# Two rows sent to all partitions through scratch memory instead of through diagonals and products with ones, in a decoder layer of 16 sequences

## The reference

```python
x = layernorm(x + linear_attention(x))                 # 16 heads of 32, elu+1, causal cumulative sums
x = layernorm(x + channel_attention(q=x, k=ctx, v=ctx))
x = layernorm(x + expert_ffn(x))                       # one of 8 experts for each sequence, 512 -> 2048 -> 512
# channel_attention, 4 heads of 128 channels, for (global, local):
scores = einsum('bhdn,bhen->bhde', (q*wq + bq) heads, (k*wk + bk) heads) * 512**-0.5
attn = softmax(scores)                                 # 128 x 128 per head
out += einsum('bhde,bhen->bhdn', attn, (v*wv + bv) heads)
result = 2 * out * wp + bp
```

## Time and profile before

| | |
|---|---|
| median of 3 runs | 2603.87 us (2602.91 to 2604.93) |
| profiled execution | 2608.33 us |
| its span | 2606.6 us |
| TensorE busy | 2471.1 us, 95% |
| VectorE busy | 1751.3 us, 67% |
| ScalarE busy | 1172.8 us, 45% |
| GpSimd busy | 532.9 us, 20% |
| mean granted TensorE clock | 0.979 |

### The profile page before, as it was taken

One profiled execution on the slowest core, in us unless ns is written; L12 is line 12 of the kernel. 1 busy time (PEld: TensorE's weight loads), 2 busy tenths in 40 slices (PEclk: granted clock), 3 DMA queues, 4 the chain that ended last, 5 costly groups with the idle time before them and its releaser, 6 DMA issues.

```text
span 2606.6 us, 33240 instructions
## 1 busy us (share of the span) xinstructions
PE 2471.1 (95%) x11584; PEld 1988.0 (76%) x11584; DVE 1751.3 (67%) x2721; ACT 1172.8 (45%) x1920; POOL 532.9 (20%) x452
## 2 busy tenths in 40 slices
PE   6866899999999999999999999999999999999998
PEld 5654678878787787878878787887878778777876
DVE  6667576677767667676767768667776766765443
ACT  4323444534444453554544454354444445354443
POOL 3132212122122212211221122212212221222110
PEclk9977999999999999999999999999999999999999
DMA  7323343433434344343433434343343434222331
GB/s 270 121 97 110 125 143 112 136 134 118 155 103 169 102 137 150 103 150 116 154 117 125 143 124 154 113 143 125 114 157 111 157 109 147 94 89 82 109 109 65
DMA packets 83400, 331.85 MB, mean 127 GB/s; under 512 B 11810, under 2 KB 11810, under 8 KB 72738
## 3 DMA queue, kind: packets, MB, share of 16 engines
q1 hardware_dynamic: 83234, 329.72, 36.6%
HBM read 306.61 MB, written 23.07 MB: 126 GB/s over the span
## 4 chain that ended last, share of the span: by engine, by line
PE 85%; DVE 9%; issue 3%; ACT 2%; DMA 1%; POOL 0%; SPq 0%; ACTq 0%; DVEq 0%; POOLq 0%
PE m L870 27%; PE h_ps L870 25%; PE acc L1047 24%; DVE junk_v L724 2%; PE m L1005 2%; PE m L946 2%; DVE a_v L728 2%; PE m L1021 1%; PE m L918 1%; PE m L953 1%; DVE h_lo L770 1%; PE m L994 1%; ACT rden_all L508 1%; DVE rden L609 1%; DVE we_lo L762 0%
## 5 line engine op out<-in xcount | busy, mean ns | idle before, releaser
L870 PE MATMUL m<-xT_hi,wq 128*128 128x512 f32 x1536 | 522.3, 404 | 25.0 <-DVE wq L552 10.7
L426 ACT ACTIVATE we_hi<-raw 128x1024 fp32r<-128x1024 f32 x256 | 271.1, 1059 | 517.8 <-PE acc L1047 512.7
L762 DVE TENSOR_TENSOR we_lo<-raw,we_hi 128x1024 fp32r<-128x1024 f32 x256 | 368.7, 1440 | 187.1 <-ACT we_hi L426 187.1
L1047 PE MATMUL acc<-we_hi,h_hi 128*128 128x512 f32 x1024 | 425.7, 416 | 0.4
L870 PE MATMUL h_ps<-x2T_hi,we_hi 128*128 128x512 f32 x1024 | 409.0, 399 | 5.9 <-DVE x2T_lo L756 5.9
L870 PE MATMUL h_ps<-x2T_lo,we_hi 128*128 128x512 f32 x1024 | 405.0, 395 | 0.0
L870 PE MATMUL h_ps<-x2T_hi,we_lo 128*128 128x512 f32 x1024 | 404.9, 395 | 0.0
L1047 PE MATMUL acc<-we_hi,h_lo 128*128 128x512 f32 x1024 | 404.7, 395 | 0.0
L1047 PE MATMUL acc<-we_lo,h_hi 128*128 128x512 f32 x1024 | 404.3, 395 | 0.0
L436 ACT ACTIVATE hid<-h_ps,b 128x512 f32<-128x512 f32 x256 | 175.6, 686 | 475.6 <-PE h_ps L870 475.6
L870 PEld LDWEIGHTS m<-xT_hi,wq 128*128 128x128 f32 x1536 | 294.6, 192 | 98.9 <-issue 27.4
(11 more groups left out here) (126 smaller groups left out, 3486.1 us busy)
## 6 DMA issues: line engine op xcount, KB each, us to landing
raw<-in_w SPq DMA_DIRECT2D x256, 512.0 KB, 3.8
wq<-wq_scratch SPq DMA_DIRECT2D x180, 512.0 KB, 3.3
xT_raw<-in_xT SPq DMA_DIRECT2D x16, 1024.0 KB, 5.8
x<-in_x_tok SPq DMA_DIRECT2D x16, 1024.0 KB, 5.5
ctx_tok<-in_ctx_tok SPq DMA_DIRECT2D x16, 1024.0 KB, 4.8
ctx_T<-in_ctxT SPq DMA_DIRECT2D x16, 1024.0 KB, 4.9
out_dram<-x SPq DMA_DIRECT2D x16, 1024.0 KB, 4.8
wq_scratch<-wq SPq DMA_DIRECT2D x12, 512.0 KB, 4.5
```

Of the source, the lines that this page charges most:

```text
L426: act.activation(we_hi[:, g % NW, :], raw[:, g % NR, :], ACT.Copy).then_inc(whi_done, 1)
L762: dve.tensor_tensor(we_lo[:, g % NW, :], raw[:, g % NR, :], we_hi[:, g % NW, :].bitcast(F32), ALU.subtract).then_inc(wlo_done, 1)
L870: last = pe.matmul(out, lhsT, rhs, start=(n == 0), stop=(n == 3 * len(pairs) - 1))
L1047: last = pe.matmul(acc[t][:, :], hx[:, f % 2, ts], wx[:, g % NW, C:], start=(f == 0 and n == 0), stop=(f == FC - 1 and n == 2))
```

## The change

The two rows take another way. `c_col` and `k_all2` are each stored by SP, element by element, as a row of 512 in DRAM scratch, and read back with one broadcast DMA to all 128 partitions, into `c_sb` and `const_b`. The diagonals on GpSimd, the two products with ones on TensorE and ScalarE's two copies out of PSUM go. ScalarE's four sums move from h = 4 to h = 1. SP gets a store at h = 2 and a read at h = 4 for the sums, a store at h = 18 and a read at h = 20 for the constants. The waits follow.

```diff
--- before.py
+++ after.py
@@ -53,6 +53,9 @@
+    c_dram = nc.dram_tensor("c_scratch", [1, XH * P], F32, kind="Internal").ap()
+    k_dram = nc.dram_tensor("k_scratch", [1, XH * P], F32, kind="Internal").ap()
     with ExitStack() as ctx:
@@ -95,7 +98,6 @@
         c_sb = sb("c_sb", [P, XH, P])
-        diag = sb("diag", [P, XH, P])
         s_x, s_q = sb("s_x", [P, XH]), sb("s_q", [P, 2, XH])
@@ -149,12 +151,12 @@
         x1_done, x2_done, norm_done = sem("x1_done"), sem("x2_done"), sem("norm_done")
-        g_mm, sx_mm, c_mm, cb_done = sem("g_mm"), sem("sx_mm"), sem("c_mm"), sem("cb_done")
-        csum_done, diag_done, sx_done, sq_done = sem("csum_done"), sem("diag_done"), sem("sx_done"), sem("sq_done")
+        g_mm, sx_mm, c_st, c_in = sem("g_mm"), sem("sx_mm"), sem("c_st"), sem("c_in")
+        csum_done, sx_done, sq_done = sem("csum_done"), sem("sx_done"), sem("sq_done")
         sc_done, max_done, nmax_done, exp_done = sem("sc_done"), sem("max_done"), sem("nmax_done"), sem("exp_done")
         rec_done, rec2_done, av_done = sem("rec_done"), sem("rec2_done"), sem("av_done")
-        asum_done, kall_done, kall2_done, diag2_done = (sem(n) for n in ("asum_done", "kall_done", "kall2_done", "diag2_done"))
-        aT_mm, kb_mm, aT_done, kb_done, x1c_done = (sem(n) for n in ("aT_mm", "kb_mm", "aT_done", "kb_done", "x1c_done"))
+        asum_done, kall_done, kall2_done = (sem(n) for n in ("asum_done", "kall_done", "kall2_done"))
+        aT_mm, k_st, aT_done, k_in, x1c_done = (sem(n) for n in ("aT_mm", "k_st", "aT_done", "k_in", "x1c_done"))
         out_mm, res2_done = sem("out_mm"), sem("res2_done")
@@ -217,6 +219,31 @@
                             load_job(a + 1, j + NQ - JOBS)
+                    if h == 2 and inside(c):
+                        sp.wait_ge(csum_done, XH * c + XH)
+                        if (due := upto(c - 1, 16, 16)) is not None:
+                            sp.wait_ge(c_in, due)
+                        sp.dma_start(c_dram[0].rearrange("(h p) -> p h", p=P), c_col[:, :], allow_slow_non_contiguous=True).then_inc(c_st, 16)
+                    if h == 4 and inside(c):
+                        sp.wait_ge(c_st, 16 * c + 16)
+                        if (due := upto(c - 1, 12, 4)) is not None:
+                            sp.wait_ge(sc_done, due)
+                        sp.dma_start(c_sb[:, :, :].rearrange("p h e -> p (h e)"), c_dram.broadcast_to([P, XH * P])).then_inc(c_in, 16)
+                    if h == 18 and inside(c):
+                        sp.wait_ge(kall2_done, c + 1)
+                        if (due := upto(c - 1, 16, 16)) is not None:
+                            sp.wait_ge(k_in, due)
+                        sp.dma_start(k_dram[0].rearrange("(h p) -> p h", p=P), k_all2[:, :], allow_slow_non_contiguous=True).then_inc(k_st, 16)
+                    if h == 20 and inside(c):
+                        sp.wait_ge(k_st, 16 * c + 16)
+                        sp.wait_ge(csum_done, XH * c + XH)
+                        if (due := upto(c - 1, TT, TT)) is not None:
+                            sp.wait_ge(x1c_done, due)
+                        sp.dma_start(const_b[:, :], k_dram.broadcast_to([P, C])).then_inc(k_in, 16)
                     if h == 11 and inside(z):
@@ -309,10 +336,6 @@
-            def diagonal(col, done):
-                pool.tensor_tensor(diag[:, :, :], ident[:, :].unsqueeze(1).broadcast_to([P, XH, P]),
-                                   col[:, :].unsqueeze(2).broadcast_to([P, XH, P]), ALU.mult).then_inc(done, 1)
             for i in range(NB + 4):
@@ -321,12 +344,6 @@
                                        b2[:, 0:1, :].broadcast_to([P, TT, C]), ALU.add).then_inc(b2_done, 1)
-                if inside(c):
-                    pool.wait_ge(csum_done, XH * c + XH)
-                    if (due := upto(c - 1, 1, 1)) is not None:
-                        pool.wait_ge(kb_mm, due)
-                    diagonal(c_col, diag_done)
                 if inside(e):
@@ -340,11 +357,7 @@
                 if inside(c):
-                    pool.wait_ge(kall2_done, c + 1)
-                    pool.wait_ge(c_mm, c + 1)
-                    diagonal(k_all2, diag2_done)
-                    pool.wait_ge(kb_done, c + 1)
+                    pool.wait_ge(k_in, 16 * c + 16)
@@ -444,6 +457,18 @@
                     split_x2(b, 3)
+                if h == 1 and inside(c):
+                    act.wait_ge(ctxT_in, 16 * c + 16)
+                    if (due := upto(c - 1, 16, 16)) is not None:
+                        act.wait_ge(c_st, due)
+                    if (due := upto(c - 1, TT, TT)) is not None:
+                        act.wait_ge(x1c_done, due)
+                    for hd in range(XH):
+                        if (due := upto(c, XH, hd)) is not None:
+                            act.wait_ge(csum_done, due)
+                        act.activation(const_b[:, :], ctx_T[:, hd, :], ACT.Copy,
+                                       accum_out=c_col[:, hd:hd + 1]).then_inc(csum_done, 1)
                 if i == 0 and h in JOB_AT:
@@ -454,24 +479,6 @@
                     normalise(1, e)
-                if h == 4 and inside(c):
-                    act.wait_ge(ctxT_in, 16 * c + 16)
-                    if (due := upto(c - 1, 1, 1)) is not None:
-                        act.wait_ge(diag_done, due)
-                    if (due := upto(c - 1, TT, TT)) is not None:
-                        act.wait_ge(x1c_done, due)
-                    for hd in range(XH):
-                        if (due := upto(c, XH, hd)) is not None:
-                            act.wait_ge(csum_done, due)
-                        act.activation(const_b[:, :], ctx_T[:, hd, :], ACT.Copy,
-                                       accum_out=c_col[:, hd:hd + 1]).then_inc(csum_done, 1)
-                if h == 5 and inside(c):
-                    act.wait_ge(c_mm, c + 1)
-                    if (due := upto(c - 1, 12, 4)) is not None:
-                        act.wait_ge(sc_done, due)
-                    act.activation(c_sb[:, :, :], by_head, ACT.Copy).then_inc(cb_done, 1)
                 if h == 7 and inside(c):
@@ -515,11 +522,6 @@
                     high_part(a, 1)
-                if h == 21 and inside(c):
-                    act.wait_ge(kb_mm, c + 1)
-                    act.wait_ge(csum_done, XH * c + XH)
-                    act.activation(const_b[:, :], M2[:, :], ACT.Copy).then_inc(kb_done, 1)
                 if h == 22 and inside(a):
@@ -674,7 +676,7 @@
             def scores_ctx(c):
-                dve.wait_ge(cb_done, c + 1)
+                dve.wait_ge(c_in, 16 * c + 16)
                 for v, bq in enumerate((BQG, BQL)):
@@ -732,8 +734,8 @@
                         dve.wait_ge(kall_done, c + 1)
-                        if (due := upto(c - 1, 1, 1)) is not None:
-                            dve.wait_ge(diag2_done, due)
+                        if (due := upto(c - 1, 16, 16)) is not None:
+                            dve.wait_ge(k_st, due)
                         dve.tensor_tensor(k_all2[:, :], k_all[:, :], cols[:, BP, :], ALU.add).then_inc(kall2_done, 1)
@@ -946,16 +948,10 @@
-            def ctx_sums(c):
-                pe.wait_ge(diag_done, c + 1)
-                pe.wait_ge(sc_done, 12 * c + 2)
-                pe.matmul(by_head, ones[:, :], diag[:, :, :], start=True, stop=True).then_inc(c_mm, 1)
             def x_sums(c):
-                pe.wait_ge(cb_done, c + 1)
+                pe.wait_ge(sc_done, 12 * c + 2)
                 for h in range(XH):
@@ -987,18 +983,10 @@
-            def constants(c):
-                pe.wait_ge(diag2_done, c + 1)
-                pe.wait_ge(aT_done, c + 1)
-                pe.matmul(by_head, ones[:, :], diag[:, :, :], start=True, stop=True).then_inc(kb_mm, 1)
             def attend(c, t):
                     pe.wait_ge(ctxT_in, 16 * c + 16)
-                    pe.wait_ge(kb_done, c + 1)
                 else:
@@ -1059,8 +1047,6 @@
                     gram(c)
-                if h == 5 and inside(c):
-                    ctx_sums(c)
                 if h == 7 and inside(c):
@@ -1078,8 +1064,6 @@
                     spread_reciprocal(a, 2 * (h - 20) + 1)
-                if h == 21 and inside(c):
-                    constants(c)
                 if 23 <= h <= 26 and inside(a):
```

## The result

The changed kernel takes 2627.19 us (median of 6 runs, 2624.24 to 2630.08) against 2604.4 us for the kernel before (6 runs, 2601.99 to 2610.7). The ratio is 1.0082, 95% interval [1.0068, 1.0096]: slower by 0.8%. The forecast was 2561, with a range of 2543 to 2583.

A forecast was written before the change was run, and what follows sets the result against it. TensorE was taken as the bound, busy 2471.1 of 2606.6 us and 85% of the chain. Products 24.8, edges 16.7 and projection wait 2 summed to 43.5, say 43 us gained: 2561 us, range 2543 to 2583.

The forecast's parts named there:

- the queue: DMA queue: two 256 KB reads and two 2 KB stores add 3% an iteration, no chain engine waiting there; cost nothing.
- the store's price: Store of 512 single elements: 5 us to landing, bounds 3.9 and 21.2; may take 12 us before anything is late.
- Rival 3: Late element store delays VectorE's residual 2 and TensorE; slower, 2678 us, deciding from about 15 us of store; chance 0.09.
- stays above 153.3: Sign in the profile after: a steady period above 153.3 us, not 152.5, means freed time is partly given back.
- rival 1: GpSimd's adds hit more VectorE low parts, TensorE waits at the projection; 20 us gained, 2584 us; chance 0.13.
- The rule of the Trainium skill: At the element stores: a strided last dimension becomes one descriptor per element, here 512, making the 21.2 us bound the one to watch.
- Products with ones: Two TensorE products removed from the steady iteration: 1.05 and 0.86 us, 24.8 us gained over 13 iterations.
- ScalarE's sums in half step 1: Four ScalarE sums, 3.0 us, moved from half step 4 into 4.30 us of idle time; cost nothing.
- The contention at the low parts: GpSimd's adds beside VectorE's low parts: the 1.53 us wait before the projection stays nearly; 0.2 us an iteration, 2 in all.
- rival 2: The constants' row comes early enough that GpSimd's adds no longer collide with VectorE; 67 us gained, 2537 us; chance 0.07.
- Edges: Iterations i = 1, 2 and 16: diagonal waits and products go; 16.7 us gained, ends 6.2 and 21.9.
- GpSimd loses two diagonals, off the chain: GpSimd: the two removed diagonals were taken as off the chain, with no gain put on them.

The follow-up runs named there:

- kernel 7: Changed kernel with both stores' 512 single elements written 64 bytes apart and the rows read from an input, not scratch; 2555.41 us.
- kernel 1: Changed kernel with both stores as 128 runs of 16 bytes instead of 512 single elements, rows permuted; 2555.98 us, ratio 0.9805 to the kernel before.
- kernel 3: Changed kernel with only the constants through scratch; the sums keep diagonal, product and copy, ScalarE's sums stay at half step 4; 2675.67 us.
- kernel 4: Changed kernel with both element stores issued by ScalarE on its own queue, the reads staying with SP; 2628.2 us, ratio 1.0089 to the kernel before.
- kernels 2 to 5: Changed kernel with only sums through scratch (2584.34 us), only constants (2675.67), stores on ScalarE's queue (2628.2), stores on GpSimd's queue (2619.4).
- kernel 6: Changed kernel, but TensorE transposes the columns to four rows, ScalarE copies them behind its query features, stores write four 512 B runs; 2603.78 us.

## Why the prediction was wrong

**The step that failed is the sentence on *the queue***: "in a stretch where no engine on the chain waits for a load: nothing". It priced the new DMAs by their bytes (3%) and put the rest at nothing. The store holds up the loads behind it, on every queue tried: the raw load lands 3 to 5 us after the store has. So a raw load that used to land with room to spare was late at ScalarE, and by ScalarE's order at the projection: 2.83 us of idle and 2.41 of slow clock, 5.2 us an iteration, 68 in all. The rule for such a row is to ask who needs the loads *behind* it, and by when.

**Beside it, *the store's price* was mis-sized.** It took 5 us for the store, with bounds of 3.9 and 21.2; it measured 9.5 to 11.1. By the prediction's own path that alone would have changed little: nothing is late before 12 us, and so it was. GpSimd's adds started at 1176.80, 16.3 us after VectorE had `k_all2` (1160.49); the forecast had 11.1 (1163.9 less 1152.84). They were five us behind, and residual 2 still didn't wait for them in the steady iterations (three waits of VectorE for GpSimd's adds in the whole run, and none in the iteration shown).

**Rival 3 had the culprit and the wrong path.** It named the late element store and put it on the constants' own row, deciding from about 15 us of store. It decided at 10 to 11 us, by way of another load. Its chance of 0.09 was too low: with bounds of 3.9 to 21.2, nothing in the trace made 5 more likely than 10. The sign "stays above 153.3" came true (157.1), but it was written for rival 1, whose path this wasn't.

**The rule of the Trainium skill pointed the right way for a reason that didn't hold here.** The Trainium skill ("DMA: Bandwidth & Descriptors", "Rules for kernel authors") warns of one descriptor per element. The trace agrees that such a store is to be avoided; kernel 7, with the same 512 descriptors and 2.6 us, shows that here their number isn't what costs.

**The rest of the sum held.** *Products with ones*: 1.91 us an iteration, as taken; kernel 1's period of 151.7 bears it out. *ScalarE's sums in half step 1*: no price seen. *The contention at the low parts*: TensorE's wait before the projection is 1.38 us in kernel 1 (1.53 before), 0.15 an iteration against 0.2 forecast; the store of 2.8 us didn't open rival 2. *Edges*: 16.7 forecast, 10 in the changed kernel, and 20.7 in kernel 1 (its profiled span is 58.3 shorter, 37.6 of that between the Gram products of i = 3 and 16). *Not foreseen*: the second diagonal. "GpSimd loses two diagonals, off the chain" was written of GpSimd alone, while the same text had GpSimd's adds slowing VectorE: 0.8 us an iteration, some 10 in all. It stood in the 2.35 us in which TensorE was idle: 1.53 before the projection, and 0.74 at the transposes, which the prediction passed over.

Kernel 1, with a store that is quick, took 2556.0 us against the forecast of 2561. That is not a hit of the whole sum: in its own group it gained 52.4 us against 43.5, and most of the surplus of 8.9 is the diagonal.

**Open.** What in the path to memory makes the sixteenth neighbour dear isn't shown; the trace shows the loads' packets stretched, and has no record below the DMA engine. No run tells neighbours as such from neighbours written by different DMA engines. Nor is it shown why a raw load is held 12.2 us in kernel 3 and 10.6 in the changed kernel, or why `xT_raw` ahead of the store is held in some iterations of kernel 4 and not in others.

## What to carry to other kernels

Price a small store by where its pieces fall, not by its bytes: columns of [128, 4] written as single elements into one dense row took about 10 us here, and the same data in runs of 16 bytes, or as single elements 16 or 64 bytes apart, 2.6 to 4.7. Look up every load that is issued or still in flight while such a store is under way, on any queue, and when its reader needs it; that reader need have nothing to do with the change. And when a helper's work on GpSimd goes away, look at what VectorE was doing at that moment.

## What the runs showed of the hardware

- A 2 KB DMA of 512 neighbouring 4-byte writes has a median of 9.5 to 11.7 us to landing in kernels 2 to 5 and the changed one, whichever engine issues it. A 512 KB load issued after it, on its queue or another, takes 10.6 to 12.2 us where the median is about 4. The store's own packets take 0.4% of the engines' time; the load's packets of 4 KB take 1.9 us each in place of 0.16 (kernel 4).
- The form decides (store of the constants): 2.6 us for 1 write per 64 bytes, 2.8 to 3.2 for 4, 4.0 for 8, 9.5 for 16.
- The clock behind an idle time of TensorE: after 1.38 and 1.53 us the next 12 matmuls took 3.04 (granted clock 1.00); after 4.36 us they took 5.45 (0.51). After 1.84 us a Gram product took 3.81 (1.00) in nine steady periods of kernel 6 and 5.44 (0.68) in three.
- GpSimd slows VectorE: a diagonal of 1.08 us beside it turned 0.54 us of VectorE's work into 1.32.
